# A graph kernel on one Trainium2 core: the edge gathers are issued against SyncE's answers, two gathers behind

## What is computed

```
# layer 0: attention over edges, summed per destination (segment softmax over d = dst)
w = sum(q[s] * k[d]) / sqrt(25);  alpha = softmax of w per destination
out = segment_sum(alpha[:, None] * x[s], d)
# layer 1: weighted sum of table rows, per receiving node
out = segment_sum((x @ W)[edge_col] * edge_val[:, None], edge_row) + b
```

## Time and profile before

| | us |
|---|---|
| median of 3 runs | 8288.19 |
| the profiled execution | 8300.19 |
| its span, first to last instruction | 8298.5 |
| mean granted TensorE clock | 0.796 of full speed |

### The profile page before, as it was taken

How to read it: one execution, slowest core, us unless ns; L and a number is a source line. 1 busy time by engine, 2 the same in 40 slices (tenths; PEclk the granted TensorE clock), 3 DMA queues, 4 the chain that set the end, 5 groups by cost and what they waited for, 6 DMA issues and landing times. The chain is left out here.

```text
span 8298.5 us, 129786 instructions
## 1 busy us (share of the span) xinstructions
PE 5030.9 (61%) x23474; PEld 3877.8 (47%) x23475; DVE 3712.8 (45%) x14369; ACT 1845.1 (22%) x4706; POOL 4735.0 (57%) x5589
## 2 busy tenths in 40 slices
PE   0464666666666667776288777654445444444499
PEld 0353544545554545555266666543333333333377
DVE  6463444444555555555554424433333333333445
ACT  6111333333333333333122222210000000000044
POOL 2576646665555555555566556656666666666500
PEclk9886767787778888888689988877777777777799
DMA  3100003333333333333100000013333333333200
GB/s 87 34 4 6 3 13 89 90 89 87 84 85 84 81 81 84 82 82 80 36 3 4 20 17 3 3 32 91 91 91 91 91 91 91 91 91 92 74 25 18
DMA packets 505323, 495.45 MB, mean 60 GB/s; under 512 B 374862, under 2 KB 402135, under 8 KB 504407
## 3 DMA queue, kind: packets, MB, share of 16 engines
q0 software_dynamic: 200192, 432.72, 19.1%
q1 hardware_dynamic: 154712, 33.52, 2.2%
q10 hardware_dynamic: 150271, 27.46, 1.9%
HBM read 463.03 MB, written 30.23 MB: 59 GB/s over the span
## 5 line engine op out<-in xcount | busy, mean ns | idle before, releaser
L1847 POOL DMA_INDIRECT XN<-table,XN x3128 | 2984.5, 954 | 985.6 <-issue 917.4
L585 POOL DMA_INDIRECT records<-slot_rec,slot_pos x1564 | 1573.5, 1006 | 942.9 <-SPq L541 531.2
L2159 PE MATMUL gcn_psE<-XN,gcn_pE 128*125 x3520 | 1125.0, 484 | 1213.3 <-DVE gcn_pE L2175 922.9
L2159 PEld LDWEIGHTS gcn_psE<-XN,gcn_pE 128*125 128x125 f32 x3520 | 825.8, 243 | 1512.5 <-issue 1352.2
L1978 PE MATMUL gat_psE<-XN,gat_pE 128*125 x3520 | 1112.8, 470 | 190.2 <-ACT gat_pE L2034 171.2
L1978 PEld LDWEIGHTS gat_psE<-XN,gat_pE 128*125 128x125 f32 x3520 | 784.3, 234 | 351.9 <-issue 206.2
L2187 DVE TENSOR_TENSOR X<-X,gcn_psE 125x256 f32 x440 | 184.3, 419 | 1537.3 <-remote 1077.6
L76 POOL TENSOR_TENSOR cell<-cell 1x1 int32<-1x1 int32 x874 | 162.7, 186 | 1174.7 <-remote 505.4
L2241 ACT ACT_TABLE_LOAD x1 | 1.3, 1283 | 2345.0 <-PEq L118 2345.0
L1970 PE MATMUL gat_psP<-ident,XN 125*128 125x125 f32 x1760 | 325.7, 316 | 324.3 <-ACT gat_sc L2030 211.2
L2175 DVE TENSOR_SCALAR gcn_pE<-iota_n,gcn_lk,gcn_rec 128x125 f32<-128x125 f32 x1760 | 502.8, 362 | 16.0
(11 more groups left out here) (454 smaller groups left out, 8178.0 us busy)
## 6 DMA issues: line engine op xcount, KB each, us to landing
XN<-table,XN POOLq DMA_INDIRECT x3128
records<-slot_rec,slot_pos POOLq DMA_INDIRECT x1564
XN<-records SPq DMA_DIRECT2D x782, 6.0 KB
gat_rec<-records ACTq DMA_DIRECT2D x440, 6.0 KB
gcn_rec<-records ACTq DMA_DIRECT2D x440, 6.0 KB
table<-XN ACTq DMA_DIRECT2D x5, 1250.0 KB
table<-room ACTq DMA_DIRECT2D x25, 250.0 KB
out_x<-X SPq DMA_DIRECT2D x25, 250.0 KB
```

The costliest lines, as they stand in the source:

```text
L585: pool.indirect_dma_start(out=rec_d[1], out_offset=bass.IndirectOffsetOnAxis(ap=slot_pos[:, h, j:j + 1], axis=0), in_=slot_rec[:, h, j, :] ...
L1847: pool.indirect_dma_start(out=rows_t[:, s, j, :], out_offset=None, in_=table, in_offset=bass.IndirectOffsetOnAxis(ap=rec_g[:, s, j, 1:2].b ...
L2159: last = pe.matmul(psE[d][0:B, 0:D], pE[:, d, j, :], rows_t[:, slot_of(g), j, :].rearrange("p a w -> p (a w)"), start=(j == 0), stop=(j == ...
```

## The change

`edge_walk` gets two semaphores, `issued` and `seen`. Before each gather POOL now waits until `seen` is above the number of the gather and counts `issued`. SP answers the first two gathers of group g - 3, then waits for the arrival of group g - 4 and counts `arrived`, then answers the last two gathers of group g - 3. `seen` starts at 2, as in `Turns`. Nothing else is touched.

```diff
@@ edge_walk
-            arrived, used, settled = (sem(f"{name}_{x}") for x in ("arrived", "used", "settled"))
+            arrived, used, settled, issued, seen = (sem(f"{name}_{x}") for x in ("arrived", "used", "settled", "issued", "seen"))
...
+                def answer(t, s, half):
+                    with loop(sp, SUB // 2) as j:
+                        sp.wait_ge(issued, t * (RING * SUB) + (s * SUB + half * (SUB // 2) + 1) + j)
+                        sp.sem_inc(seen, 1)
+
                 def body(t, s):
                     load_records(sp, t * RING + s, rec_g[:, s, :, :], group_ready[s])
+                    if near(t, s, 1 - LAG):
+                        answer(*near(t, s, 1 - LAG), 0)
                     if near(t, s, -LAG):
                         arrive(*near(t, s, -LAG))
-
+                    if near(t, s, 1 - LAG):
+                        answer(*near(t, s, 1 - LAG), 1)
+
+                sp.sem_inc(seen, Turns.AHEAD)
                 each_group(sp, body)
                 for g in range(NG - LAG, NG):
+                    if g + 1 < NG:
+                        answer((g + 1) // RING, (g + 1) % RING, 0)
                     arrive(g // RING, g % RING)
+                    if g + 1 < NG:
+                        answer((g + 1) // RING, (g + 1) % RING, 1)
...
                     for j in range(SUB):
+                        pool.wait_ge(seen, t * (RING * SUB) + (s * SUB + j + 1))
+                        pool.sem_inc(issued, 1)
                         pool.indirect_dma_start(out=rows_t[:, s, j, :], out_offset=None, in_=table,
```

## The result

The changed kernel takes 8385.46 us (median of 14 runs, 8338.65 to 8412.44), the kernel before on the same chips 8302.66 us (14 runs, 8277.54 to 8334.47): a ratio of 1.0098, 95% interval 1.0084 to 1.0112. It is slower by 1%, where 0.3% less was forecast. The profiled execution of the changed kernel took 8387.71 us.

The account below looks back on a forecast made before the run. No engine was full; full-ring pauses held the edge sums, steps through PE, DVE and ACT the softmax. 8300.19 + 7 - 32 = 8275 us, less 12 for the median: 8263 us, 8 in 10 between 8030 and 8450.

Parts of the forecast that it names:

- The extra instructions on POOL: POOL's added wait and count: 0.01 us per gather, 16 us in the edge sums, hidden by the ring's wait in the softmax.
- The wait for SP's answer: POOL held before gathers: 0.206 us each, taken from stage a; edge sums 5.93 us a group for 5.92, +7 us.
- pauses of the two kinds: Edge sums: pauses from SP's silence replace those from the full ring; if both added up, +338 us.
- the 0.85 us a group: Edge sums before the change: 5.92 us a group less 5.07 undisturbed, read as pauses ahead of the settle instruction.
- SP's program: I cost all this at 0: Both edge stages: loads and arrival counts queued behind SP's new waits cost 0, SP having time for four answers a group.
- The second rival: SP becomes the bound: +81 us in the sums, +81 in the softmax, with the 7 us +169, 8457 us; chance 0.27.
- Softmax, -32 us: Softmax over edges: forced pauses inside a group free PE's counts sooner, -32 us, between bounds of -193 and +193.
- One in six: Softmax: estimated share taken of the -193 us due if every remote wait of DVE ended one pause earlier.
- The third rival: Both edge stages: SP always answers in time, only 0.01 us per gather is left, +16 us, 8304 us; chance 0.08.
- Remote waits of DVE of some 9 us still there: Sign of a right forecast: in the edge sums DVE's remote waits keep their length of some 9 us.
- The first rival: Early pauses free PE's counts sooner: -164 us in sums, -160 in softmax at full strength; 8048 us expected; chance 0.35.
- The rule of the page: Rapid semaphore increments from one engine can block another; by it 6256 added increments would make stalls more frequent. Not adopted.

Follow-up runs that it names:

- POOL's half alone: Against the kernel before, both stages: POOL waits for `seen`, set high from the start, and counts `issued`; SP answers nothing. Ratio to before 1.0082.
- the leads: How many gathers SP's answer may be behind: exchange in the softmax alone with 1 (0.9854 of before) or 2 (0.9930); in both stages with 4 (1.0194).
- written-out answers: Against the changed kernel, SP's loops of two answers are replaced by straight code: 1.0116 of before in both stages, 1.0087 with the exchange in the softmax alone.
- lead 1: Exchange in the softmax alone, `seen` starting at 1 where the changed kernel has 2: 8183.46 us, 0.9854 of before.
- lead 24: The changed kernel with SP's answer allowed to be 24 gathers behind in place of two, both stages: 1.0557 of before.

## Why the prediction was wrong

*The extra instructions on POOL: right in the sums, open in the softmax.* In the sums +16 us were put down and none can be seen (5.92 against 5.93). In the softmax they were to "vanish in the ring's wait"; they stand behind it (0.62 for 0.46 us after a ring wait). The kernel with POOL's half alone reads some 25 us longer there, at a lower clock, so the price is not settled.

*"The wait for SP's answer", 0.206 us per gather from stage a: the term that was mis-sized.* The sum was 5.93 us a group, measured 6.30; by the prediction's own sum, 5.07 + 4 x (0.01 + wait), the wait is 0.30 us. Times 391 groups that is +149 us for +7. That pauses of the two kinds would replace each other and not add up was right (the ring's 243.2 us went to 5.9), and so was the place of the new idle time. The size was not the property of the exchange that I took it for, but of SP's program around it, which is another in the edge stages. A smaller slip: the 0.85 us a group that the prediction calls pauses ahead of the settle instruction are 0.68 by its rows (228.4 us in 338 groups). Nothing in the sum hangs on it.

*"SP's program: I cost all this at 0": the step that failed.* Its ground was that SP waited 1886.1 us for landings, "so it has time for four answers a group". That row lists only part of SP's waits, as the view's line for the softmax, 1400 to 3800 us, does with 251 of 343:

```profile
SPq L1827 <- DMA XN<-table,XN: 1526.0, 251, 14.1
```

SP had more time than the row says, 4.4 us a group in the sums. What was left out is the price of what it was given. Eighteen instructions more a group made its program 4.1 us longer, from 1.48 to 5.56 us, and POOL needs 5.07 for a group. The price was to be had from the trace of before: in the stretch of stage a that the forecast rests on, SP's program takes 1.34 us per scatter of 1.48 by the single records, and SP waits only 0.15. Four answers at that price are 5.3 us a group (an estimate), more than was idle. So stage a was itself a stretch in which SP had next to nothing to spare. The second rival had the mechanism, "SP becomes the bound", with its mark met: over 1.50 us a gather, measured 1.576. Its price was 81 us in the sums on top of the 7, measured 149 in all; its other half, the same again in the softmax, had the wrong sign.

*Softmax, -32 us: the direction right, under half of the size.* 70 us less from first gather to last. The reason given, a forced pause in the middle of a group that frees the others sooner, is supported by the leads (6.71, 6.83 and 7.09 us a group for 1, 2 and 4, the last on another chip) and by the written-out answers, which force hardly a pause and gain nothing. "One in six" was a guess; had the size come out, it would have been luck.

*The third rival, that the wait never binds: wrong in the whole change* (311 waits for SP in the sums), and nearly right for the kernel with the answers written out there, with 134 waits and 0.04 us a group.

*"Remote waits of DVE of some 9 us still there" in the sums: wrong.* They fell to 3.0 us each. The first rival said under 6 us and had that right; its payoff, 164 us, did not come, since the same wait came back as PE waiting for an arrival and POOL for an answer. The rule of the page "VectorE: DVE Perf Modes", section "The TRN2 errata", in the Trainium skill, speaks of a deadlock and of increments on completion; as the prediction stretched it, to stalls and to counts by instructions of their own, it would have made the added counts themselves the cost. Against that stand the 1564 counts added on POOL, which cost the sums nothing (5.92), and all 3128 of that stage with the answers written out, at 0.04 us a group. By these runs the count isn't the price here, the loops around it are.

## What to carry to other kernels

Before work is put on an engine that seems idle, price that work in the engine's own time, and hold the sum against the pace of the very stretch where it will run: here 4.1 us a group were added to 1.48, where POOL needs 5.07. That the engine waits a lot is not enough, and a view of its waits may list only some of them. When an exchange between engines was late here, loosening it only moved the lateness to the next thing the slow engine owed; a shorter program (no loop of two) took most of the cost away in the sums. And the throttle paid only where the throttled engine has slack: the same code gained 0.7 to 1.0% in the stage that other engines pace, more with lead 1 (1.5%), and lost 1.5% in the stage that POOL paces.

## What the runs showed of the hardware

A late answer was of use: in the softmax the exchange helps while SP is slow, by 0.12 to 0.24 us a group, and with the answers written out the gain is gone. With loops of two rounds on SP the sums lost about 0.17 to 0.19 us a group for each loop, and with the same two answers written out some 0.02. The exchange of one count each way, in a loop and with the loads beside it, took SP 1.34 us per scatter in stage a. The granted clock moved with the kernels and not only with the chip, from 0.774 (lead 24) to 0.802 (lead 1); how much of the softmax's gain and of the loss with POOL's half alone it carries was not separated. What the slow spells are, and whether anything but POOL's silence ends them, stays open.
